# The late tiles of a sparse graph attention planned in two batches, their scan spread over 22 units in place of 18

## The reference

```python
h = jnp.maximum(_layernorm(x), 0.0)
h = jnp.einsum('ni,hif->hnf', h, W)
s1 = jnp.einsum('hnf,hf->hn', h, a1);  s2 = jnp.einsum('hnf,hf->hn', h, a2)
scores = leaky_relu(s1[:, :, None] + s2[:, None, :], 0.2)
scores = jnp.where(adj[None] > 0, scores, NEG_BIG)
out = jnp.einsum('hnm,hmf->hnf', softmax(scores), h)      # heads side by side: (N, 512)
return x + elu(out)
```

## Time and profile before

| | |
|---|---|
| median of 3 runs | 799.62 us (799.23 to 802.81) |
| profiled execution | 800.83 us, its span 799.0 us |
| mean granted TensorE clock | 0.848 of full speed |
| busy over the span | TensorE 71%, VectorE 83%, ScalarE 59%, GpSimd 54% |
| DMA over the span | 269.51 MB, 337 GB/s on average |
| edge stage, from about 370 us | VectorE scans until 638 us, works on edges to 783.8 us |

### The profile page before, as it was taken

The page is one execution under the profiler, slowest core; times in us unless marked ns, Lnnn a source line. Parts: engine busy times, 40 slices in busy tenths (PEclk is TensorE's granted clock), DMA queues, the critical chain, the costliest instruction groups (busy, mean ns, idle before and its releaser), DMA issues.

```text
span 799.0 us, 9153 instructions
## 1 busy us (share of the span) xinstructions
PE 570.9 (71%) x2182; PEld 406.0 (51%) x2182; DVE 659.7 (83%) x2066; ACT 470.2 (59%) x695; POOL 427.6 (54%) x804
## 2 busy tenths in 40 slices
PE   0489788998788887653777686857476759977770
PEld 0245444554444444343556565646465648766650
DVE  4659988999876777764879999999699989999861
ACT  0778888799999899235265665657354223333321
POOL 4634444534432332237666467557467776887830
PEclk9989999999987889755888779787697679998895
DMA  9999998899999999319999999999999887999995
GB/s 288 420 356 392 359 356 346 334 396 419 415 422 418 421 421 421 138 55 343 349 373 409 402 420 385 409 399 402 396 389 281 241 254 196 269 269 276 285 256 109
DMA packets 65130, 269.51 MB, mean 337 GB/s; under 512 B 12145, under 2 KB 12145, under 8 KB 52786
## 3 DMA queue, kind: packets, MB, share of 16 engines
q1 hardware_dynamic: 38706, 190.53, 59.7%
q0 software_dynamic: 26368, 78.36, 33.0%
HBM read 243.49 MB, written 25.37 MB: 336 GB/s over the span
## 4 chain that ended last, share of the span: by engine, by line
DVE 22%; issue 11%; PE 8%; POOL 6%; DMA 6%; ACT 2%; another core or an unknown queue 2%; POOLq 0%; DVEq 0%; ACTq 0%
DVE nodes L1116 7%; DMA nodes<-table,list_column 5%; POOL nodes L959 3%; DVE places L250 3%; POOL nodes L954 2%; PE psP L1254 2%; DVE agg L1128 2%; PE psP L1255 2%; DVE best L239 2%; PE psP L1261 1%; PE psP L1262 1%; PE psC L1238 1%; ACT packed L229 1%; DVE owner L1050 1%
## 5 line engine op out<-in xcount | busy, mean ns | idle before, releaser
L651 PE MATMUL psH<-sb_W,normedT 128*128 128x512 f32 x384 | 225.5, 679 | 0.0
L229 ACT ACTIVATE packed<-adj_rows,eight 128x3072 uint8<-128x3072 int32 x66 | 188.7, 2859 | 2.1 <-issue 1.4
L954 POOL DMA_INDIRECT nodes<-table,column x138 | 139.7, 1012 | 75.7 <-issue 39.8
L1254 PE MATMUL psP<-nodes,ident 128*128 128x256 f32 x276 | 105.9, 472 | 55.0 <-issue 43.0
L959 POOL DMA_INDIRECT nodes<-table,list_column x109 | 112.0, 1027 | 58.4 <-issue 31.7
L1116 DVE TENSOR_TENSOR nodes<-nodes,psW 128x2048 f32<-128x2048 f32 (+4 forms) x66 | 138.7, 2143 | 4.2 <-ACT psW L1026 4.2
L698 POOL TENSOR_TENSOR sb_node_sum<-sb_node_sum,h_rows 128x512 f32<-128x512 f32 x48 | 61.2, 1274 | 150.9 <-ACT h_rows L616 150.9
L652 PEld LDWEIGHTS psS<-sb_Wa,normedT 128*128 128x128 f32 x384 | 78.6, 205 | 103.7 <-issue 103.7
L250 DVE FIND_INDEX8 places<-best,packed 128x8 uint32<-128x96 f32 (+6 forms) x240 | 110.5, 469 | 0.0
L239 DVE MAX8 best<-packed 128x8 f32<-128x96 f32 (+6 forms) x240 | 103.3, 463 | 6.2 <-ACT packed L229 6.1
L1255 PE MATMUL psP<-nodes,ident 128*128 128x264 f32 x276 | 102.7, 460 | 0.0
(11 more groups left out here) (177 smaller groups left out, 924.9 us busy)
## 6 DMA issues: line engine op xcount, KB each, us to landing
adj_rows<-in_adj_dram SPq DMA_DIRECT2D x66, 1536.0 KB
sb_adj_rows<-in_adj_dram SPq DMA_DIRECT2D x30, 1536.0 KB, 11.6
table<-h_rows SPq DMA_DIRECT2D x48, 260.0 KB, 7.5
sb_x_rows<-in_x_dram SPq DMA_DIRECT2D x48, 256.0 KB, 7.7
result<-in_x_dram POOLq DMA_DIRECT2D x19, 512.0 KB
out_dram<-result SPq DMA_DIRECT2D x19, 512.0 KB
result<-in_x_dram POOLq DMA_DIRECT2D x10, 256.0 KB
out_dram<-result SPq DMA_DIRECT2D x10, 256.0 KB
```

The source lines that it names most:

```text
L229: nc.scalar.activation(words.bitcast(mybir.dt.uint8), sb["adj_rows"][buffer_of(i)][:], ACT.Square, bias=sb["eight"][:], scale=-17.0, accum ...
L651: nc.tensor.matmul(psH[:, t % 2], normedT[:, t % 2, kc], sb["W"][:, kc], start=(kc == 0), stop=(kc == KC - 1))
L954: nc.gpsimd.indirect_dma_start(out=nodes[:, node_at[u] + i * w.direct + j], out_offset=None, in_=table, in_offset=bass.IndirectOffsetOnAxi ...
L1254: nc.tensor.matmul(low, sb["ident"][:], nodes[:, n, 0:LOW], start=a, stop=False)
```

## The change

The planner gets a second due time. The 144 scan items are spread over `later - 6` = 28 - 6 = 22 rounds in place of 18. The late tiles are planned in two batches: tiles 30 to 37 (counted at the end of iteration `scanned_in[38]` = 10, placed at the end of iteration 11, `late_planned` = 1, wanted by unit 24) and tiles 38 to 47 (counted at the end of iteration 22, placed at the end of 23, `late_planned` = 2, wanted by unit 28). TensorE's `look_up(14)` and later ones wait for the first, `look_up(26)` and later ones for the second. The rule for the round of a pack is not changed. The diff, where repetitions of the same slicing are left out:

```diff
+SPLIT = 38
...
     late = next(u for u, w in enumerate(UNITS) if w.tile >= EARLY)
-    COUNTED = late - 6
+    later = next(u for u, w in enumerate(UNITS) if w.tile >= SPLIT)
     dve_items = [(t, n) for t in range(EARLY, TILES) for n in range(2 * len(segments_of(t)))]
-    dve_round = spread_over([scan_cost(*item) for item in dve_items], COUNTED)
+    dve_round = spread_over([scan_cost(*item) for item in dve_items], later - 6)
...
+    batches = [(EARLY, SPLIT, E, E + SPLIT - EARLY, scanned_in[SPLIT], late), (SPLIT, TILES, E + SPLIT - EARLY, V, later - 6, later)]
+    assert batches[0][4] <= late - 6
...
-                if u == late:
-                    pool.wait_ge(late_planned, 1)
+                for b, batch in enumerate(batches):
+                    if u == batch[5]:
+                        pool.wait_ge(late_planned, b + 1)
...
-                if u == late:
-                    act.wait_ge(late_planned, 1)
+                for b, batch in enumerate(batches):
+                    if u == batch[5]:
+                        act.wait_ge(late_planned, b + 1)
...
-            def count_late():
+            def count_late(b):
 
+                t0, t1, v0, v1, _, _ = batches[b]
-                info, s, flags = sb["infoC"], SLOTS["C"], sb["flags"]
-                dve.wait_ge(sb["cut_step"], cut_count(TILES))
-                dve.wait_ge(sb["checked"], 2 * TILES)
+                info, s, flags, mine = sb["infoC"], SLOTS["C"], sb["flags"], slice(v0 - E, v1 - E)
+                places = slice(v0 - FIRST["C"], v1 - FIRST["C"])
+                dve.wait_ge(sb["cut_step"], cut_count(t1))
+                dve.wait_ge(sb["checked"], 2 * t1)
                 dve.wait_ge(late_cleared, 1)
-                did(nc.vector.tensor_scalar(used[:], info[:, E0:E0 + LV, 0:s], 0.0, None, ALU.is_gt))
+                did(nc.vector.tensor_scalar(used[:, mine], info[:, places, 0:s], 0.0, None, ALU.is_gt))
...
-            def place_late():
+            def place_late(b):
...
+                dve.wait_ge(late_placed, b + 1)
...
-                nc.vector.tensor_reduce(worst[:], flags[:], AX.X, ALU.max).then_inc(worst_ready, 1)
+                if v1 == V:
+                    nc.vector.tensor_reduce(worst[:], flags[:], AX.X, ALU.max).then_inc(worst_ready, 1)
...
-                if u == COUNTED:
+                if u == later - 6:
                     rank_last(nc, dve, sb, TILES - 1)
-                    count_late()
-                if u == COUNTED + 1:
-                    place_late()
+                for b, batch in enumerate(batches):
+                    if u == batch[4]:
+                        count_late(b)
+                    if u == batch[4] + 1:
+                        place_late(b)
...
-                if u > COUNTED + 3:
-                    pe.wait_ge(late_planned, 1)
+                planned = sum(u > batch[4] + 3 for batch in batches)
+                if planned:
+                    pe.wait_ge(late_planned, planned)
...
-                if u == COUNTED:
-                    pe.wait_ge(late_counted, 1)
+                for b, (_, _, v0, v1, counted, _) in enumerate(batches):
+                    if u != counted:
+                        continue
+                    pe.wait_ge(late_counted, b + 1)
                     pe.wait_ge(facts_done, u + 4)
...
+                    n, mine = v1 - v0, slice(v0 - E, v1 - E)
+                    nc.tensor.matmul(psC[:, 0:n], sb["earlier"][:], listed[:, mine], start=True, stop=True)
+                    nc.tensor.matmul(psC[:, n:2 * n], sb["ones"][:], listed[:, mine], start=True, stop=True).then_inc(late_placed, 1)
```

More of the change, by code:

```diff
@@ L849, in attend_edges @@
     E = next(k for k, v in enumerate(VISITS) if v.tile >= EARLY)
-    LV, E0 = V - E, E - FIRST["C"]
+    LV = V - E
+    batches = [(EARLY, SPLIT, E, E + SPLIT - EARLY, scanned_in[SPLIT], late), (SPLIT, TILES, E + SPLIT - EARLY, V, later - 6, later)]
+    assert batches[0][4] <= late - 6
     def ring(size):
@@ L1152, in count_late @@
                 dve.wait_ge(late_cleared, 1)
-                did(nc.vector.tensor_scalar(used[:], info[:, E0:E0 + LV, 0:s], 0.0, None, ALU.is_gt))
-                for v0, v1 in runs(E, V, lambda v: v.direct):
-                    d = VISITS[v0].direct
-                    did(nc.vector.tensor_scalar(falling[:, v0 - E:v1 - E, 0:d], info[:, v0 - FIRST["C"]:v1 - FIRST["C"], 0:d],
+                did(nc.vector.tensor_scalar(used[:, mine], info[:, places, 0:s], 0.0, None, ALU.is_gt))
+                for a, z in runs(v0, v1, lambda v: v.direct):
+                    d = VISITS[a].direct
+                    did(nc.vector.tensor_scalar(falling[:, a - E:z - E, 0:d], info[:, a - FIRST["C"]:z - FIRST["C"], 0:d],
@@ L1163, in count_late @@
-                did(nc.vector.tensor_tensor(listed[:], degree[:], sb["taken"][:, E:V], ALU.subtract))
-                did(nc.vector.tensor_scalar(empty[:], degree[:], 0.0, None, ALU.is_equal))
+                did(nc.vector.tensor_scalar(late_sums[:, mine], late_sums[:, mine], -64.0 * N, None, ALU.add))
+                did(nc.vector.tensor_tensor(listed[:, mine], degree[:, mine], sb["taken"][:, v0:v1], ALU.subtract))
+                did(nc.vector.tensor_scalar(empty[:, mine], degree[:, mine], 0.0, None, ALU.is_equal))
@@ L1169, in count_late @@
+                did(nc.vector.scalar_tensor_tensor(flags[:, t0:t1], degree[:, mine], 17.0, late_sums[:, mine],
                                                    ALU.mult, ALU.not_equal))
-                dve.wait_ge(late_counted, 1)
-                did(nc.vector.tensor_scalar(half[:], listed[:], 0.5, None, ALU.mult))
+                dve.wait_ge(late_counted, b + 1)
+                did(nc.vector.tensor_scalar(half[:, mine], listed[:, mine], 0.5, None, ALU.mult))
                 settle()
-                did(nc.vector.tensor_scalar(sb["column"][:, E:V], falling[:], float(N + 1), None, ALU.min))
@@ L1174, in count_late @@
-                did(nc.vector.tensor_tensor(sb["half_sq"][:, E:V], half[:], half[:], ALU.mult))
-            def place_late():
-                info, s, flags = sb["infoC"], SLOTS["C"], sb["flags"]
-                settle()
[L1180 to L1183, removed]
-                for v0, v1 in runs(E, V, lambda v: v.rest):
-                    did(nc.vector.tensor_scalar(flags[:, TILES + v0:TILES + v1], psC[:, LV + v0 - E:LV + v1 - E],
-                                                float(P * VISITS[v0].rest), None, ALU.is_gt))
+                did(nc.vector.tensor_scalar(sb["column"][:, v0:v1], falling[:, mine], float(N + 1), None, ALU.min))
@@ new lines, in count_late @@
+                did(nc.vector.tensor_tensor(sb["half_sq"][:, v0:v1], half[:, mine], half[:, mine], ALU.mult))
+            def place_late(b):
+                _, _, v0, v1, _, _ = batches[b]
+                info, s, flags, n = sb["infoC"], SLOTS["C"], sb["flags"], v1 - v0
+                places = slice(v0 - FIRST["C"], v1 - FIRST["C"])
+                settle()
+                dve.wait_ge(late_placed, b + 1)
+                did(nc.vector.scalar_tensor_tensor(sb["neg_centre"][:, v0:v1], psC[:, 0:n], 1.0, half[:, v0 - E:v1 - E], ALU.mult, ALU.add))
+                did(nc.vector.tensor_tensor(info[:, places, s:s + 1], psC[:, 0:n].unsqueeze(2), sb["taken"][:, v0:v1].unsqueeze(2), ALU.subtract))
+                for a, z in runs(v0, v1, lambda v: v.rest):
+                    did(nc.vector.tensor_scalar(flags[:, TILES + a:TILES + z], psC[:, n + a - v0:n + z - v0],
+                                                float(P * VISITS[a].rest), None, ALU.is_gt))
```

14 lines of the change are left out of this document (5 added, 9 removed).

## The result

The changed kernel took 823.0 us (median of 4 runs, 821.55 to 825.54), beside 800.1 us for the kernel before: a ratio of 1.0296, with a 95% interval of 1.0259 to 1.0333. That is **3% slower**, where +20.3 us and a median of 820.5 us had been forecast. The profiled execution took 823.04 us with a span of 821.5 us, 22.5 us longer than before.

What follows compares the result with a forecast made beforehand. The prediction took VectorE to bound the kernel nearly everywhere, so its idle time and added work decide. It summed 2.8 + 6.5 + 21 - 7.0 - 3.0 = +20.3 us to 820.5 us, with a range of 808 to 831 us.

Steps and rivals of the forecast that it cites:

- the waits of the cut rounds: ScalarE's packs wait for the search of tile t - 2 in 12 rounds, idling VectorE: +21 us, between 17 and 25.
- second plan: Added `count_late` and `place_late` instructions on VectorE's path: +2.8 us, between 2.3 and 3.1.
- first batch's wait: Iteration 11's end: `look_up(14)` waits for the placing, delaying ScalarE's packs and VectorE's weigh: +6.5 us, between 1.3 and 8.
- hole ahead of unit 14: VectorE's 7.02 us wait for gathers before unit 14's scores is given back: -7.0 us, between -7 and -3.
- tail: GpSimd starts its last stretch four units later, shrinking gather waits at unit 32: -3.0 us, between -3.5 and 0.
- The bound: VectorE is the bound nearly everywhere, so the change is worth its effect on VectorE's idle time plus added work.
- The second batch's 0: Second batch's wait equals the one of before, four units later, with no packs due: 0 us.
- Round 1: First of the 12 cut rounds, six items left to cover the wait: 0.2 us of idle time.
- upper bound of 50 us: Upper bound of the packs' waits: 12 rounds at 4.2 us each, the idle time seen in iteration 2.
- Rival 1: Adjacency traffic is the real bound and spreading it pays: -7 us, about 792.5 us; chance 0.07.
- Rival 2: Waits of the 12 rounds are hidden, the first batch's is not: -0.7 us, about 799 us; chance 0.10.
- rival 3: Waits plus a new traffic jam at units 14 to 18, and no gain in the tail: 830.5 us; chance 0.13.

Runs made afterwards that it cites:

- the first series: First of three measuring series: third place, whole tiles, two batches and early place of the plan, each in its own kernel; the kernel before had 795.0 us.
- the third place: Changed kernel with a third place for packed tiles, so packs wait for the search of t - 3: 1.0038 (803.1 us), then 1.0053 in the third series.
- the early place: Changed kernel with `place_late` of each batch moved ahead of `weigh`, from behind the scan items: ratio 1.0131, 810.6 us.
- two batches on the 18 rounds: Changed kernel's two batches on the 18 whole-tile rounds of before: ratio 1.0073, 805.9 us; with `place_late` ahead of `weigh` as well, 0.9922.
- the kernel before with the early place: Kernel before (one batch, 18 rounds) with only `place_late` moved ahead of `weigh`: ratio 0.9951, then 0.9948 in the third series.
- both repairs: Changed kernel with a third place for packed tiles and `place_late` ahead of `weigh`: ratio 1.0084, then 0.9993 in the third series.

## Why the prediction was right

The time was inside the range and 2.5 us from the forecast. The mechanism was right too: the largest term, the waits of the cut rounds, was forecast and measured to 1.2 us, and in none of the 11 rounds that show it is the forecast off by more than 0.5 us. Three of the other terms are off by 1 to 2 us each, partly in opposite directions; that the sum fits this closely is in part luck. By its own steps, in us of the trace:

| step | forecast | measured |
|---|---|---|
| second plan | +2.8 | +1.7 |
| first batch's wait | +6.5 | +7.7 |
| waits of 12 cut rounds | +21 | +19.8 |
| hole ahead of unit 14 | -7.0 | -7.0 |
| tail | -3.0 | -1.0 |
| sum | +20.3 | +21.2 |

The span grew by 22.5 us; the last 1.3 are small differences, among them 2 us more idle time between iterations 1 and 2 (4.21 us for ScalarE's facts, before 2.17 at a cut step). Both come with a wait of ScalarE put down to something remote (below), and the first series, in whose traces there is no such wait, shows neither.

- *The bound* was read right: VectorE's idle time, and hardly anything else, decides.
- *The second plan*: `count_late` took 1.8 us a batch, `place_late` 0.6 and 0.7, together 4.8 in place of 3.1. The instructions over half the tiles save more than I took: the reduction of `late_used` took 0.29 and 0.32 us in place of 0.45.
- *The first batch's wait*: the chain was as forecast, `facts_out`, pack, grow, pack, exp. The term was 1.2 us short because I scaled the look-up from the wrong count: the four matmul instructions of 1.04 us were two lists with two passes each, so six lists are twelve instructions and took 2.75 us, not 1.6. The second batch's 0 held: its one row of 2.22 us stands for the 1.31 us and another 1.06 us behind the late sums of before.
- *The 12 rounds*: 11 show idle time that is new. Those with three items left cost most, as forecast: 2.33, 2.74, 2.27 and 2.89 us. ScalarE's own waits were longer than the 3 to 5 us forecast, 5.9 us on average. The third place shows that it is this wait: the same rounds without it are some 21 us faster by the ratios of either pair of measurements. Round 1 is different. The prediction took the 4.20 us in iteration 2 of the kernel before for a first case of this wait, and its upper bound of 50 us rests on that. It was the exp behind two packs, but no search held the packs up: the facts ahead of them came late, after 12.20 us put down to something remote, and in the changed kernel it was the same, 13.20 us and then 4.23 us. The trace of the early place in the first series has no such wait and shows the price of round 1 itself, 0.84 us where 0.2 was forecast, and 12 waits of packs, 77.2 us in sum; two batches on the 18 rounds have no wait in iteration 2 at all. The first line is of the kernel before, the second of the early place:

```profile
396.60 0.28 ACT L1002 ACTIVATE facts<-psC 128x126 f32<-128x126 f32 x1 [12.20 <-remote]
```

```profile
396.61 4.49 DVE L1122 TENSOR_TENSOR nodes<-nodes,psW 128x1024 f32<-128x1024 f32 x2 [0.84 <-ACT psW L1032]
```

- *The hole* went as forecast, but what took it away is not shown. It is no fixed price: the kernel before with the early place had 4.24 us ahead of unit 14 in one trace, and in the other nothing there and 7.17 us ahead of unit 15 (first line). Two batches on 18 rounds, with the traffic of before, have no wait ahead of unit 14 either, and 0.81 us ahead of unit 15 where iteration 10 waits, 1.78 us where it does not (second line). So the batch's wait is not needed to make it small. The nine traces with 22 rounds have at most 0.99 us ahead of units 14 to 16. What the smaller traffic does alone was not tried.

```profile
583.96 0.21 DVE L1095 TENSOR_TENSOR score<-nodes,s 128x48 f32<-128x48 f32 x1 [7.17 <-issue]
```

```profile
578.30 0.24 DVE L1101 TENSOR_TENSOR score<-nodes,s 128x48 f32<-128x48 f32 x1 [1.78 <-DMA nodes<-table,list_column]
```

- *The tail* was mis-sized. The gathers' 2.95 us went, but `finish` then waits for `grow` in each of the last iterations, 1.5 us where VectorE had been held up by the gathers before. Taking one of two waits away at the same place gave only what it was longer.
- *Rival 1* (traffic is the bound, the spread pays) fell: from 396 to 532 us the changed kernel moved 350 GB/s with the DMA engines 96% busy, in place of 392 at 100%, the waits for gathers are gone, and yet with both repairs the spread is worth nothing. By the Trainium skill (DMA: Bandwidth & Descriptors, Specifications), with its 435 GB/s for the fabric and about 358 for one core from HBM, the argument had been that the stage is as full as it can be. The trace does not agree with the second figure, which it exceeds with 392 GB/s, and it is 10% short of the first; and while VectorE scans, the kernel before waited for gathers at one unit only. *Rival 2* (waits hidden) fell by the rows above, *rival 3* (a new hole at units 14 to 18) by the absence of a wait for gathers there.

## What to carry to other kernels

A buffer rule such as "pack t once t - 2 is searched" holds a phase, and not only an order: it was free because the planner's rounds were whole tiles, and it cost 20 us once the same planner cut tiles across rounds. Before items are spread anew, put every wait between two engines into the table of rounds and look for pairs that fall into the same round, with what stands behind the waiting instruction on its in-order engine. And where a shared tile makes one engine wait for another's reading, read early in the iteration: moving three lines up gave 0.5%, more than all that was to be had from the spread.

## What the runs showed of the hardware that was not expected

The traces differ by waits that the profile puts down to something remote: up to 13.5 us ahead of ScalarE's facts, up to 3.3 us on VectorE. Nearly all come while adjacency rows are loaded. With what was queued behind them they took about 16 us of VectorE's time in the worst trace, and the four traces of the first series have none. The third place alone had none in the first series and four on ScalarE in the third, so they are no matter of the code alone; but where they come, they come at the same places: a wait of 11.8 to 13.5 us ahead of the facts that iteration 2 wants is in all ten other traces.

The Trainium skill (Runtime: NRT & Kernel Launch, Instruction fetch mechanics) says that engines fetch their instructions in blocks by DMA, mostly hidden. Such a fetch behind a full queue could look like this, but the traces do not bear it out: the profile records the packets of the instruction queues, and within the 12.16 us wait of the version with both repairs, from 563.35 to 575.51, there is none; the next comes at 576.1. In the 12.39 us wait of the same kernel's other trace one lies 1.5 us ahead of the end, in the 12.20 us wait of the kernel before 7 us ahead. What the waits are stays open.

Three kernels measured twice agree between series within 0.3%, or 2 us, and the fourth, with both repairs, differs by 0.9%. So a difference of less than 1% between series says little here.
